# Turning chunk 2's queries and keys at block 4 instead of block 7 of the first head group

## The reference

```python
qkv = ternary_linear(x, w_qkv)
q, k = (rms_norm(q), rms_norm(k))
q = apply_rotary_emb(q, cos, sin)
k = apply_rotary_emb(k, cos, sin)
...
scores = jnp.where(causal, einsum('bqhgd,bkhd->bhgqk', qg, k) * scale, -inf)
attn = softmax(scores, axis=-1)
y = einsum('bhgqk,bkhd->bqhgd', attn, v)
return ternary_linear(rms_norm(y), w_proj)
```

## Time and profile before

| what | us |
|---|---|
| median of 3 runs | 567.24 |
| lowest and highest | 566.35, 568.52 |
| the profiled execution | 565.76 |
| its span, first to last instruction | 564.0 |
| TensorE busy with matmuls | 475.9 |
| ScalarE busy | 356.8 |
| VectorE busy | 312.0 |

### The profile page before, as it was taken

The page is one execution under the profiler, slowest core; times in us unless marked ns, Lnnn a source line. Parts: engine busy times, 40 slices in busy tenths (PEclk is TensorE's granted clock), DMA queues, the critical chain, the costliest instruction groups (busy, mean ns, idle before and its releaser), DMA issues.

```text
span 564.0 us, 9883 instructions
## 1 busy us (share of the span) xinstructions
PE 475.9 (84%) x3202; PEld 265.7 (47%) x3202; DVE 312.0 (55%) x881; ACT 356.8 (63%) x557; POOL 185.2 (33%) x244
## 2 busy tenths in 40 slices
PE   1486969999899996999998987969978799999970
PEld 1473322333233331333333442427867698988860
DVE  6976326643762219613157365386886266665637
ACT  3246759998899985999887755554432255555520
POOL 3722102016646035850311025034155024443420
PEclk9988779999999998999999878898979899999995
DMA  7121013533890449713369312037213334443349
GB/s 204 35 56 42 10 34 105 157 87 102 201 279 10 107 128 322 211 38 84 99 207 371 163 41 73 1 84 167 69 50 110 97 84 123 122 123 114 94 161 333
DMA packets 61243, 69.09 MB, mean 122 GB/s; under 512 B 12259, under 2 KB 53443, under 8 KB 60579
## 3 DMA queue, kind: packets, MB, share of 16 engines
q1 hardware_dynamic: 57499, 58.74, 36.8%
q0 software_dynamic: 3408, 9.34, 4.6%
q10 hardware_dynamic: 288, 0.39, 0.3%
HBM read 32.68 MB, written 26.22 MB: 104 GB/s over the span
## 4 chain that ended last, share of the span: by engine, by line
PE 51%; DVE 18%; issue 8%; ACT 8%; DMA 7%; SPq 5%; POOL 1%; another core or an unknown queue 1%; ACTq 0%; DVEq 0%; POOLq 0%
PE ps L1599 16%; PE ps L1579 11%; ACT prob L815 6%; PE ps L1781 6%; PE ps L1800 3%; PE ps L1726 2%; PE ps L1519 2%; PE ps L1635 2%; PE ps L1649 2%; PE ps L1608 1%; PE ps L1540 1%; PE ps L1804 1%; SPq L383 1%; PE ps L1772 1%; DVE y_sb L1465 1%
## 5 line engine op out<-in xcount | busy, mean ns | idle before, releaser
L815 ACT ACTIVATE prob<-ps 128x1024 f32<-128x1024 f32 (+3 forms) x320 | 260.2, 920 | 60.2 <-PE ps L1579 58.6
L1599 PE MATMUL ps<-prob,v_sb 128*32 128x512 f32 (+3 forms) x1280 | 159.2, 572 | 7.2 <-POOL prob L659 6.0
L1579 PE MATMUL ps<-qk 64*128 64x512 f32 (+3 forms) x640 | 122.5, 448 | 15.0 <-DMA qk<-qT 6.7
L659 POOL TENSOR_SCALAR_AFFINE_SELECT prob<-prob 128x512 f32<-128x512 f32 x64 | 42.4, 665 | 212.8 <-ACT prob L815 211.8
L1579 PEld LDWEIGHTS ps<-qk 64*128 64x128 f32 x640 | 54.8, 195 | 112.4 <-ACT prob L815 87.1
L751 POOL DMA_INDIRECT pair_out<-yo,xg x39 | 37.9, 972 | 66.0 <-DVE yo L1445 65.7
L1599 PEld LDWEIGHTS ps<-prob,v_sb 128*32 128x32 f32 x1280 | 26.0, 110 | 54.5 <-issue 34.4
L1103 DVE COPY o_sb<-ps 128x512 f32<-128x512 f32 x16 | 11.1, 691 | 59.3 <-PE ps L1599 59.0
L1726 PE MATMUL ps<-x2T,ws 128*128 128x512 f32 (+1 forms) x144 | 39.7, 428 | 0.9 <-DVE hid L1322 0.9
L712 POOL DMA_INDIRECT rows_by_expert<-xs,slots x32 | 31.4, 981 | 18.9 <-DVE slots L1286 10.2
L1090 DVE CAST qT<-ps 96x512 fp32r<-96x512 f32 x16 | 11.0, 686 | 41.2 <-PE ps L1540 41.2
(11 more groups left out here) (193 smaller groups left out, 701.9 us busy)
## 6 DMA issues: line engine op xcount, KB each, us to landing
qk<-qT SPq DMA_DIRECT2D x138, 64.0 KB, 2.1
w_parts<-parts SPq DMA_DIRECT2D x16, 352.0 KB
w<-w_parts SPq DMA_DIRECT2D x2, 2816.0 KB, 14.3
xg<-rows_by_expert SPq DMA_DIRECT2D x39, 129.0 KB
yfin<-pair_out SPq DMA_DIRECT2D x8, 512.0 KB, 7.3
raw<-in_w SPq DMA_DIRECT2D x8, 352.0 KB
w_parts_d<-parts SPq DMA_DIRECT2D x16, 176.0 KB
w_parts<-w_parts_d SPq DMA_DIRECT2D x1, 2816.0 KB
```

Of the source, the lines that this page charges most:

```text
L659: nc.gpsimd.affine_select(out=t, in_=t, compare_op=ALU.is_ge, fill=0.0, base=0, pattern=[[0, HPG], [1, P]], channel_multiplier=-1).then_in ...
L815: nc.scalar.activation(prob[:, u % NPB, 2 * hf:2 * hf + 2, c0:CH], ps[:, b:b + 2, c0:CH], ACT.Exp, scale=SCALE).then_inc(exp_done, 1)
L1579: ins = M(ps[:, 2 * (n % NSB) + h, c0:CH], qk[rows, par, PAIRS, kt * P:(kt + 1) * P], qk[rows, par, hf, j * CH + c0:(j + 1) * CH], start=T ...
L1599: ins = M(ps[VW * h:VW * (h + 1), O_BANK, c0:CH], v_sb[:, kt, :], prob[:, u % NPB, h, c0:CH], start=(kt == 0), stop=(u == LAST_OF[j]), ski ...
```

## The change

The entry of the first group's schedule that turns chunk 2 stands at 4 instead of 7. TensorE then issues the four transposes after the values product of block 4 (and ahead of the scores of block 7) instead of after that of block 7 (and ahead of the scores of block 10). It is still the third use of the turning bank, and still ahead of ("out", 0, 0) at 8, so all counts of semaphores and the orders of the other engines stay as they are.

```diff
 FIRST_GROUP = {
-    7: [("round", 0, 2)], 8: [("out", 0, 0)], 12: [("out", 0, 1)], 14: [("round", 0, 3)],
+    4: [("round", 0, 2)], 8: [("out", 0, 0)], 12: [("out", 0, 1)], 14: [("round", 0, 3)],
     24: [("out", 0, 2)], **{30 + 2 * r: [("round", 1, r)] for r in range(ROUNDS)}, NU - 1: [("weights",)],
 }
```

## The result

| | before | after |
|---|---|---|
| median of 11 runs each, us | 565.48 | 562.47 |
| lowest and highest | 562.01, 570.9 | 553.77, 564.07 |
| profiled execution, its span | 565.76, 564.0 | 561.11, 559.3 |

The ratio is 0.9856, with a 95% interval of 0.9807 to 0.9906: faster by 1.4%, or 8.1 us of the 565.48 (5.3 to 10.9 by the interval). It leaves out as slow every run more than 1.5% above the fastest of its kernel, which are seven of the eleven of the changed kernel and one of the kernel before. By the medians of all runs the kernel is faster by 0.5% (3.0 us), by the two profiled executions by 0.8%. The forecast was 1.1%, 6.13 us.

A forecast was written before the change was run, and what follows sets the result against it. It took TensorE and ScalarE as one pipeline, losing time in TensorE's 4.9 us wait for chunk 2. Gains of 5.23 + 0.28 + 0.62 = 6.13 us brought 567.24 to 561.1 us, range 559.0 to 564.2.

The forecast's parts named there:

- 1, wait at the new place: Behind block 4's values product, the turn finds VectorE's rotation finished with 1.51 us to spare and costs no wait.
- 2, cost of the turn there: The four transposes fall in a low clock stretch until 63.9 and charge nothing; at most 1.09 us.
- 3, wait of the first output's turn: Its 0.28 us wait for VectorE goes, so TensorE reaches block 12's scores at 70.84.
- 5, gain from round 1's turn to block 12's scores: Block 12's scores start at 70.84 instead of 76.07, a gain of 5.23 us.
- step 4: Chunk 2's data arrive 5.88 us sooner, at 70.19, 0.65 us before TensorE needs them at block 12.
- my bounds: For chunk 2's arrival: issues spaced as before give no wait; spaced like chunk 3's first four, 0.30 us.
- step 6: Behind the hole the clock stays up: 0.28 us at the first exponential plus 0.62 of ScalarE pauses; bounds 0 and 2.5.
- How the numbers follow: Chances of the cases (forecast 0.64; faster 0.84, same 0.11, slower 0.05) and the range 559.0 to 564.2 us.
- Step 7: The 6.13 us gain lasts to the kernel's end, as nothing known is tied to an absolute time.
- the clock did not stay low longer: Rival denied here: low clock from 57 lasts another 3.4 us past 63.9; gain 4.4, 562.8 us; chance 0.14.
- The slower rival: TensorE waits for VectorE's rotation at the turn's new place; 10.5 us late makes about 570.1 us; slower chance 0.05.
- The gain given back: Rival: gain lost at later meetings, such as group boundaries; 567 if all, 564.2 if half; within 0.5% chance 0.11.

The follow-up runs named there:

- after_third: The changed kernel, unedited, timed a third time on another chip than the two other repeats; ratio 0.9853 to the kernel before.
- before_again: The kernel before the change, unedited, run once more; ratio 1.0012 to the kernel before.
- after_again: The changed kernel, unedited, run once more; ratio 0.9869 to the kernel before.
- turn_at_3: The kernel before with chunk 2's turn at block 3 instead of 7; ratio 0.9989 to the kernel before.
- two edits: On the changed kernel: expert-weight pieces 6 to 8 ahead of the third group's moves, and VectorE's copy of output 1 ahead of two norm multiplications; together 0.9703.
- turn_at_5: The kernel before with chunk 2's turn at block 5 instead of 7; executed once, 49.31 us from round 1's turn to block 24's scores.
- early_loads: The changed kernel with expert-weight pieces 6 to 8 stored and loaded ahead of the third group's moves; ratio 0.9879 to the kernel before.
- turn_at_6: The kernel before with chunk 2's turn at block 6 instead of 7; executed once, 49.54 us from round 1's turn to block 24's scores.
- late_dmas: The changed kernel with chunk 2's DMAs issued only after block 10's scores; executed once, 51.54 us from round 1's turn to block 24's scores.

## Why the prediction was right, and where it was not

Point by point, distances in us:

| step | forecast | measured |
|---|---|---|
| 1, wait at the new place | 0, with 1.51 to spare | 0, with 1.52 (58.86 to 60.38) |
| 2, cost of the turn there | 0 | 0 (22.86 against 22.84 up to block 9's product) |
| 3, wait of the first output's turn | gone | gone |
| 4, wait for chunk 2 | gone, 0.65 to spare | gone, about 0 to spare (after_third: 0.97) |
| 5, gain from round 1's turn to block 12's scores | 5.23 | 28.92 - 23.64 = 5.28 |
| 6, gain from there to block 24's | 0.90 | 22.52 - 21.36 = 1.16 |
| 7, kept to the end of the attention | 6.13 | 377.1 - 370.3 - 0.3 = 6.5 |
| 7, kept to the end of the span | 6.13 | 564.0 - 559.3 = 4.7; before_again and after_again 4.3 |

The margin of step 4 follows from the queue's rows. In the kernel before the last of the nine issues was this one:

```profile
73.42 0.59 SPq L391 DMA_DIRECT2D qk<-qT  x1
```

It lay 2.65 us ahead of the start of block 12's scores (76.07). The changed kernel's last issue began at 67.78, so the data were there at about 70.43 (an estimate from these rows); TensorE arrived at 70.47. The half microsecond that one of the issues took longer had been among my bounds, and it ate most of the margin. The rest hung on the clock: step 4 took TensorE's arrival as fixed, with the low stretch on until 63.9. In after_third the clock rose early, TensorE arrived 0.97 us before the data, and the margin was not there; this wait took back what the early rise had given. Block 5, where 1.67 us of wait brought the low clock back, shows what less margin can cost.

The mechanism was as described, then, and the sum of 6.13 was 0.3 us too small, nearly all of it in step 6. ScalarE's pauses of 0.62 us went as forecast; but the 22 exponentials, whose three rows had added up to 1.94 + 3.77 + 13.71 = 19.42 us, now take 19.17 in one row, and this 0.25 I had not counted. That both parts came out so close in this pair is luck: it has its low stretches at the same places. In before_again and after_again the gain up to block 12 is 27.53 - 23.06 = 4.47 us and the one behind it 23.24 - 21.37 = 1.87. The sum, 6.34, holds again and its split does not.

What failed is the step "How the numbers follow", and in it the term "runs scatter by about 1 us to each side", which came from three runs. Over 11 runs the kernel before reaches from 562.0 to 570.9, 3.5 us below its median and 5.4 above, and the changed kernel from 553.8 to 564.1, 8.7 below and 1.6 above. The base of 567.24, a median of three, stood 1.8 us above the median of 11. The four runs on which the changed kernel's side of the ratio rests are 553.77, 556.86, 560.53 and 561.11; their middle is 558.7, just below my lower end of 559.0, while the median of all eleven, 562.47, lies inside the range. The ratio's 8.1 us likewise lie above the 7.7 that I had allowed for the gain, where the trace shows 6.44 in the stretch of the change. The range was also drawn tighter than its own terms: 567.24 - 7.7 - 1 is 558.5 and 567.24 - 5.2 + 1 is 563.0, and I wrote 559 to 562.5, as if the scatter were hardly there.

Step 7 was too sure as well. The part that it passed over with the remark that nothing there is tied to an absolute time is the one behind the attention, 182.4 to 192.9 us in fourteen traces. The profiled execution took 561.11 us and its span 559.3, where I had 559.6 and 557.9: of the 6.5 us that the changed kernel was ahead at the end of the attention, 4.7 arrived. The place of the low clock stretches differs in every execution, and the waits for gathered rows (0.4 to 5.5 us in the two traces shown) differ with the chip. Whether the change itself has a share in this loss is open, as said above.

Of the rivals: the clock did not stay low longer. It rose before 63.8 with four transposes in the stretch, as it had risen at 50.2 behind four others. The Trainium skill, "TensorE: Matmul & The Clock Gate", Part 4, says that transposes do not count as PE-busy the way matmuls do. By that rule a longer low stretch would have been the likelier case, and the traces do not bear that out. They do not refute the rule either: the transposes were 1.09 us of a stretch full of other products, and no run here shows how much they count. The slower rival's mechanism is real, but one block further on (turn_at_3). The gain given back: not in the attention; behind it 2.1 us in the first pair and 3.1 in the second, at different places, which is open.

## What to carry to other kernels

Look for a producer that has long finished when the engine in the middle picks its result up: the idle time in front of a cheap step (8.52 us before a cast) shows how far the step can be moved up, and the end of the producer shows how far not. Place such a step by the two arrivals, for here one block too early cost nearly as much as three too late, and the right block goes through with next to nothing to spare. When a hole is closed and the time hardly moves, look for the next wait inside the hole's shadow before giving the edit up: in the third group two edits worth 1.6 and 0 us apart were worth 6.5 together. And judge a gain of 1% by a distance inside the trace as well as by the total, when a part that the change doesn't touch scatters by more. Take that distance from more than one trace, and compare within one chip.

## What the runs showed of the hardware that was not expected

A wait of TensorE of only 1.67 us (turn_at_5) was followed by a low stretch of its clock, 0.50 granted over 6.8 us. The wait of 1.1 us in the second group was followed by one of 3.4 us in ten of the twelve traces that have it (in early_loads it ended at 146.5, and the clock was 0.50 from 147 to 149), but not in turn_at_6 and turn_at_5; nor was the 0.97 us of after_third. So a short wait can bring the clock down and need not.

What such a stretch costs depends first on how much of it has work to slow. In the kernel before it lay from 74.2 to 81.0, but block 12's scores started only at 76.07: 4.9 us of low clock fell on work and cost 1.15. Counted the same way, 5.1 us cost 1.2 in late_dmas, 6.4 us cost 1.9 in before_again, 6.8 us cost 2.35 in turn_at_5, 3.4 us cost 0.7 in turn_at_6, and 3.4 us cost 1.3 to 1.4 in the second group. That is 0.2 to 0.4 us for each microsecond, less than the half that an engine at half its pace would lose if it alone set the pace.

The kernel before took from 552.3 to 572.3 us over the executions of this study, with medians of 557 us on some chips and 566 on others, so that only times taken on one chip can be compared. The traces show where part of these 9 us lies: from the first to the last values product of the fourth head group it took 91.3 to 92.8 us on the faster chips and 95.2 to 98.6 on the slower ones, whatever the kernel, and the waits for gathered rows add 2 to 5 us.
